# Chunks 1 to 20 of a linear attention over 12544 positions: another order of the matrix jobs within a tile

## The chip, the core and the metric

The kernel runs on one core of a Trainium2 chip. The number that counts is the device time of one execution in microseconds (us), from launch to the last store; below it is given as the median of several executions. One further execution was recorded by the hardware profiler, and everything said here about single instructions comes from that one.

The core has five engines that work side by side and wait for each other through semaphores. TensorE (PE) multiplies matrices; its weight loads are shown as PEld. VectorE (DVE), ScalarE (ACT) and GpSimd (POOL) work on elements. SyncE (SP) starts transfers from memory. Each engine carries out its own instructions in the order of its program, so an instruction that waits holds up all that stand behind it on that engine.

## The reference

Three layers on a sequence `x` of 128 rows. Nearly all the time goes into the first, a linear cross attention that reads a context of 12544 rows:

```python
k = heads(ctx @ Wk.T + bk)              # 16 heads of 32
v = heads(ctx @ Wv.T + bv)
k_prime = relu(k @ Wkf.T) * mask        # 64 features per head
kv    = sum over rows of k_prime^T v    # 64 x 32 per head
k_sum = sum over rows of k_prime
out = (q_prime @ kv) / (q_prime @ k_sum + 1e-8)
```

The other two layers, a gated recurrence and a mixture of two experts, work on 128 rows and follow behind it.

## The kernel before, in words

Every product is made from numbers split into a high and a low part, `hi` and `lo`: three matrix multiplications (`lo*hi`, `hi*lo`, `hi*hi`; the helper `three`, L773, L774, L775) add up in one place. An engine writes the high part (a copy to a shorter type, always ACT), another the low part (the difference).

The context is worked through in **chunks** of 512 rows, `c` = 0 to 24 (the last one has half a chunk), and each chunk in four **tiles** of 128 rows, `t` = 0 to 3; tile number `n` = 4c + t, 98 in all. A tile has these jobs on PE:

- **values**: 12 multiplications 512 columns wide (weights are the context, `wv` is what moves), into the bank `v_bank`. They are for the tile's own rows.
- **keys**: 12 multiplications 512 columns wide, into `k_bank`. They are one quarter `m` = t of the keys of the *next* chunk.
- four **feature jobs**, i = 0 to 3: two multiplications of 256 columns each (L855), into the two banks `f_ps[i % 2]`.
- **key_values**: 8 multiplications of 256 columns (L868), which add this tile's, or the former tile's, features times values to `kv_ps`.

The other engines' part of a tile, by names and lines of the kernel before:

- `features_share` on ACT (L546) copies half a feature bank to `fb`; `features_sum` on DVE (L1264) adds it to the other half, into `kf`, and thereby gives the bank back (`fsum_ready`). Feature job i waits until the sum of job i-2 is done, so job 2 waits for the sum of job 0 of its own tile and job 3 for that of job 1.
- `masked_features` on DVE (L1271) applies relu and mask to the 1024 features of the tile, in place in `kf`, and raises `kf_ready`. Three instructions take it from there: `add_features` on POOL (L455) adds `kf` to `ksum_acc`; `features_high` on ACT (L552) writes the high part; `features_low` on DVE (L1277) waits for that and writes the low part, which `key_values` needs.
- `values_high` on ACT (L537), `values_low` on DVE (L1255): the split of the values.
- `keys_high` on ACT (L529, two instructions), `keys_low` on DVE (L1247, two instructions): the split of the keys, which frees `k_bank`.
- `split_ctx_high` on ACT (L521) and `split_ctx_low` on POOL (L448): the split of a tile of the context two chunks ahead. POOL does, tile by tile, `split_ctx_low` and then `add_features`.

The order is written out by hand in one program per engine. A `period` is a chunk, `tile` is a tile on ACT and on DVE. Chunks 1 to 20 are a loop of two chunks per turn on PE (`Fori`); on ACT the loop ends after chunk 18 and on DVE after chunk 16, and the rest is straight code, because chunks 17 and 18 carry four small sums each on DVE (`row_sum`) and chunks 19 to 21 the splitting of weights (`qkv_high` on ACT, `qkv_low` on DVE). Inside a loop the thresholds of the waits are computed by register instructions.

Of the kernel before, what the change touches and what calls it, by code (L numbers as in the profile page):

```python
# [13 lines left out]
CHUNK = 2 * HALF  # L14
TILES = CHUNK // P
NH_CTX = S_CTX // HALF
LAST = NH_CTX // 2
# [46 lines left out]
def perceiver_kernel(nc, x_in, ctx_in, mask_in, wq_in, bq_in, wk_in, bk_in, wv_in, bv_in, bdq_in, bdk_in,  # L64
# [5 lines left out]
    with ctx:  # L70
# [438 lines left out]
        def _(act):  # L509
# [50 lines left out]
            def tile(n, t, first=False, keys=(), splits=()):  # L560

                for i in range(2):
                    features_share(n, i, first and t == 0)
                if not (first and t == 0):
# [33 lines left out]
            def period(c, s, splits=TILES, keys=CHUNK, pieces=0):  # L598
                n = TILES * c
                for t in range(TILES):  # L600
                    tile(n + t, t, keys=((c + 1, 1 - s, t, k_bank, keys),),
                         splits=((2 * c + 4 + t // 2, s, t),) if t < splits else ())
                    if pieces:
                        qkv_high(TILES * (pieces - 1) + t)

# [43 lines left out]
            period(LAST - 1, 1, splits=0, keys=HALF)  # L649
            def weight_high(g, hs=range(2)):  # L650
# [119 lines left out]
        def _(pe):  # L770
# [41 lines left out]
            def values(n, s, t, jobs):  # L812

                for job in jobs:
                    feature_job(*job)
                pe.wait_ge(v_lo_ready, n)
                for k in range(KC):
                    value_step(n, s, t, k)
# [75 lines left out]
                    if t > 0:  # L894
                        key_values(t - 1, t + 1, first=t == 1)

            def period(c, s, n_keys=CHUNK):
                n = TILES * c
                for t in range(TILES):
                    jobs = [(c, s, n + t, t, i) for i in range(JOBS)]  # L900
                    values(n + t, s, t, jobs[0:2])
                    keys(c + 1, 1 - s, t, jobs[2:4], n_keys)
                    key_values(n + t - 1, t + 1)

# [314 lines left out]
        def _(dve):  # L1219
# [73 lines left out]
            def tile(n, t, first=False, keys=()):  # L1293

                features_sum(n, t, 0, first)
                features_sum(n, t, 1, False)
                if first and t == 0:
                    queries_out()
                else:
# [46 lines left out]
            def period(c, s, keys=CHUNK, pieces=0, sums=None):  # L1346
                n = TILES * c
                for t in range(TILES):
                    if sums is not None:
                        row_sum(sums, t)  # L1350
# [3 lines left out]
                    tile(n + t, t, keys=((c + 1, 1 - s, t, k_bank, keys),))  # L1354

            def queries_out():
                for b in range(2):
# [43 lines left out]
            dve.wait_ge(mask_loaded, 16)  # L1401
            for t in range(TILES):
                tile(t, t, first=t < 2, keys=((1, 1, t, k_bank, CHUNK),))
            with dve.Fori(1, LAST - 7, 2) as c:
                period(c, 1)
                period(c + 1, 0)
            dve.wait_ge(sums_loaded, 16 * 2)
            for i in range(2):
                period(LAST - 7 + i, 1 - i, sums=i)
            period(LAST - 5, 1, pieces=1)  # L1410
            period(LAST - 4, 0, pieces=2)
            period(LAST - 3, 1, pieces=3)
            qkv_low(3 * KC - 1)
            period(LAST - 2, 0)
            period(LAST - 1, 1, keys=HALF)
# [223 lines left out]
```

## Time and profile before

| what | us |
|---|---|
| median of three executions | 860.26 (860.06 to 860.57) |
| profiled execution, its own time | 860.48 |
| its span, first to last instruction | 858.7 |
| PE busy in it | 850.4 (99%) |
| DVE, ACT, POOL busy | 679.9 (79%), 554.5 (65%), 368.9 (43%) |

The span is what the profiler shows; about 1.8 us of launch and end lie around it. "Busy" for PE counts overlapping multiplications once. A matmul's row has the time from its start to the modelled end of its result, so rows overlap; how long one holds the engine is read from the distance between two starts.

### The profile page before, as it was taken

Reading aid. Unit: us, or ns where it says so; the run is one execution under the profiler, and the core shown is the slowest. Engines: PE = TensorE matmul, PEld = TensorE weight load, DVE = VectorE, ACT = ScalarE, POOL = GpSimd, SP = SyncE. Lnnn points to the kernel's source line nnn. Section 1 sums busy time; section 2 is a strip of 40 time slices with the busy share of each in tenths; the row PEclk is TensorE's granted clock in tenths of the full one; section 3 lists DMA queues with packets and bytes.
Section 4 is the critical chain, followed back from the end, with each engine's and each line's share of the span. In section 5 each row is a group of like instructions: output and inputs, shape, how many; then the busy total and the mean of one; then the engine's idle time right before and its main releaser. Section 6 shows DMA issues by size and latency. Waiting matters only on the chain.

```text
span 858.7 us, 14381 instructions
## 1 busy us (share of the span) xinstructions
PE 850.4 (99%) x4602; PEld 729.6 (85%) x4602; DVE 679.9 (79%) x1069; ACT 554.5 (65%) x1010; POOL 368.9 (43%) x212
## 2 busy tenths in 40 slices
PE   9999999999999999999999999999999999999998
PEld 7888888888888888888888888888888889878767
DVE  5777777777777777777777777888888878879897
ACT  5666666666666666666666666666777666587563
POOL 2555454544555544454455554445445533220000
DMA  7212214010101010010101010010101000589840
GB/s 272 98 51 73 76 52 168 24 49 24 49 24 49 24 41 33 24 49 24 49 24 49 24 49 24 28 45 25 49 25 50 26 1 1 216 319 410 306 147 13
DMA packets 19529, 66.25 MB, mean 77 GB/s; under 512 B 2224, under 2 KB 2992, under 8 KB 19120
## 3 DMA queue, kind: packets, MB, share of 16 engines
q1 hardware_dynamic: 19072, 64.88, 21.3%
q10 hardware_dynamic: 432, 1.05, 0.3%
q8 instruction: 14, 0.23, 0.1%
q14 instruction: 11, 0.09, 0.0%
HBM read 65.66 MB, written 0.26 MB: 77 GB/s over the span
## 4 chain that ended last, share of the span: by engine, by line
PE 93%; issue 4%; DVE 1%; POOL 0%; DMA 0%; ACT 0%; POOLq 0%; SPq 0%; DVEq 0%; ACTq 0%
PE side_ps L773 21%; PE side_ps L774 21%; PE side_ps L775 20%; PE kv_ps L868 11%; PE side_ps L855 11%; PE kv_ps L1165 2%; PE side_ps L965 1%; PE side_ps L971 1%; PE kv_ps L1147 1%; PE side_ps L975 1%; PE side_ps L941 1%; PE side_ps L946 0%; PE side_ps L1047 0%; PE side_ps L876 0%; DVE kv_parts L1499 0%
## 5 line engine op out<-in xcount | busy, mean ns | idle before, releaser
L455 POOL TENSOR_TENSOR ksum_acc<-ksum_acc,kf 128x1024 f32<-128x1024 f32 x97 | 233.3, 2405 | 86.7 <-DVE kf L1271 86.7
L448 POOL TENSOR_TENSOR ctx_lo<-ctx_raw,ctx_hi 128x512 fp32r<-128x512 f32 x92 | 119.3, 1298 | 273.7 <-ACT ctx_hi L521 273.7
L529 ACT ACTIVATE keys<-side_ps,bias_cols 64x512 fp32r<-64x512 f32 (+1 forms) x196 | 132.3, 675 | 149.0 <-PE side_ps L775 146.5
L1247 DVE SCALAR_TENSOR_TENSOR keys<-side_ps,bias_cols,keys 64x512 fp32r<-64x512 f32 (+1 forms) x196 | 144.9, 739 | 83.9 <-ACT keys L529 80.6
L1264 DVE TENSOR_TENSOR kf<-side_ps,fb 128x256 f32<-128x256 f32 x392 | 148.6, 420 | 16.6 <-ACT fb L546 5.3
L773 PE MATMUL side_ps<-ctx_hi,wk_lo 128*128 128x512 f32 (+1 forms) x400 | 154.2, 385 | 0.0
L773 PE MATMUL side_ps<-wv_hi,ctx_lo 128*128 128x512 f32 x392 | 153.9, 393 | 0.0
L774 PE MATMUL side_ps<-wv_lo,ctx_hi 128*128 128x512 f32 x392 | 153.8, 392 | 0.0
L774 PE MATMUL side_ps<-ctx_lo,wk_hi 128*128 128x512 f32 (+1 forms) x400 | 153.6, 384 | 0.0
L775 PE MATMUL side_ps<-wv_hi,ctx_hi 128*128 128x512 f32 x392 | 152.6, 389 | 0.0
L775 PE MATMUL side_ps<-ctx_hi,wk_hi 128*128 128x512 f32 (+1 forms) x400 | 152.4, 381 | 0.0
L546 ACT ACTIVATE fb<-side_ps 128x256 f32<-128x256 f32 x392 | 129.0, 382 | 8.5 <-PE side_ps L855 6.2
L1277 DVE TENSOR_TENSOR kf<-kf 128x1024 fp32r<-128x1024 f32 x96 | 118.3, 1232 | 12.3 <-ACT kf L552 12.3
L855 PE MATMUL side_ps<-bd,keys 128*128 128x256 f32 x784 | 126.6, 283 | 0.9 <-DVE kf L1264 0.9
L855 PEld LDWEIGHTS side_ps<-bd,keys 128*128 128x128 f32 x784 | 114.8, 190 | 9.4 <-DVE kf L1264 1.3
L537 ACT ACTIVATE v<-side_ps 128x512 fp32r<-128x512 f32 x98 | 58.7, 599 | 92.4 <-PE side_ps L775 92.4
L868 PEld LDWEIGHTS kv_ps<-kf,v 128*128 128x128 f32 x784 | 106.5, 190 | 7.6 <-issue 0.5
L868 PE MATMUL kv_ps<-kf,v 128*128 128x256 f32 x784 | 109.9, 283 | 0.3 <-DVE kf L1277 0.3
L552 ACT ACTIVATE kf<-kf 128x1024 fp32r<-128x1024 f32 x96 | 102.0, 1063 | 2.0
L1255 DVE TENSOR_TENSOR v<-side_ps,v 128x512 fp32r<-128x512 f32 x98 | 67.7, 691 | 30.0 <-ACT v L537 30.0
L775 PEld LDWEIGHTS side_ps<-ctx_hi,wk_hi 128*128 128x128 f32 x400 | 75.4, 188 | 15.1
L775 PEld LDWEIGHTS side_ps<-wv_hi,ctx_hi 128*128 128x128 f32 x392 | 73.6, 188 | 16.1
(205 smaller groups left out, 954.1 us busy)
## 6 DMA issues: line engine op xcount, KB each, us to landing
ctx_raw<-in_ctx SPq DMA_DIRECT2D x46, 512.0 KB, 3.3
early<-in_stream SPq DMA_DIRECT2D x15, 1024.0 KB, 8.4
raw<-in_stream SPq DMA_DIRECT2D x12, 1024.0 KB, 9.1
early<-in_stream SPq DMA_DIRECT2D x8, 512.0 KB, 4.3
early<-in_ctx SPq DMA_DIRECT2D x2, 512.0 KB, 6.1
early<-in_wv SPq DMA_DIRECT2D x1, 1024.0 KB, 8.0
early<-in_wq SPq DMA_DIRECT2D x1, 1024.0 KB, 9.4
early<-in_wo SPq DMA_DIRECT2D x1, 1024.0 KB, 7.0
```

Source lines behind the costliest of these rows:

```text
L448: pool.tensor_tensor(ctx_lo[:, s, :, cols], raw[:, :, t % 2 * P:(t % 2 + 1) * P], ctx_hi[:, s, :, cols].bitcast(f32), ALU.subtract).then_i ...
L455: pool.tensor_tensor(ksum_acc[:, :].rearrange("p (j f) -> p j f", f=P), ksum_acc[:, :].rearrange("p (j f) -> p j f", f=P), kf[:, t % 2, :, ...
L529: act.activation(keys_2[rows, s, 2 * m + h, 0:n], src[rows, 0:n], ACT.Identity, bias=bias_cols[rows, KC + m:KC + m + 1]).then_inc(k_hi_rea ...
L546: act.activation(fb[:, i % 2, :, :], f_ps[i % 2][:, :].rearrange("p (j x f) -> p j x f", j=2, x=2) [:, :, 1, :], ACT.Copy).then_inc(fb_rea ...
L773: pe.matmul(out_ps, st_lo, mv_hi, start=start, stop=False, **kw)
L774: pe.matmul(out_ps, st_hi, mv_lo, start=False, stop=False, **kw)
L775: return pe.matmul(out_ps, st_hi, mv_hi, start=False, stop=stop, **kw)
L855: last = pe.matmul(f_ps[i % 2][:, (j % 2) * 2 * P:(j % 2 + 1) * 2 * P], keys_2[:, s, j, t * P:(t + 1) * P], bd[:, :, :].rearrange("p x f - ...
L868: return pe.matmul(kv_ps[:, j, :, :].rearrange("p x f -> p (x f)"), v_2[:, t % 2, j, :, :].rearrange("p x e -> p (x e)"), kf_2[:, t % 2, j ...
L1247: dve.scalar_tensor_tensor(out=keys_2[other, s, 2 * m + h, 0:n], in0=src[rows, 0:n], scalar=bias_cols[rows, KC + m:KC + m + 1], in1=keys_2 ...
L1264: dve.tensor_tensor(kf[:, t % 2, 2 * i:2 * i + 2, :], f_ps[i % 2][:, :].rearrange("p (j x f) -> p j x f", j=2, x=2)[:, :, 0, :], fb[:, i % ...
L1277: dve.tensor_tensor(kf_2[:, t % 2, :, 1, :], kf[:, t % 2, :, :], kf_2[:, t % 2, :, 0, :].bitcast(f32), ALU.subtract)\
```

## The change

Only the order of work in chunks 1 to 20 (tiles 4 to 83) changes. No instruction of a tile is added or taken away.

On PE a tile was: feature jobs 0 and 1, values of this tile, the first three of the twelve multiplications of keys, feature jobs 2 and 3, the other nine, key_values of the tile in front. It becomes: feature jobs 0 and 1, key_values of the tile in front, feature jobs 2 and 3, keys, values of the *next* tile. So one values job is moved ahead of the loop, and chunk 21, which has the old order, leaves out its first one.

On ACT and DVE the split of a tile's features (`features_high`, `features_low`) moves from the middle of the following tile into the tile itself: on ACT behind the split of the context, ahead of keys_high; on DVE right behind `masked_features`, ahead of `keys_low`. POOL's and SP's programs stay as they are.

```diff
@@ ScalarE @@
+            def tile_burst(n, t, keys, splits=(), piece=None):
+                features_share(n, 0, False)
+                features_share(n, 1, False)
+                values_high(n, t, False)
+                features_share(n, 2, False)
+                features_share(n, 3, False)
+                for x in splits:
+                    split_ctx_high(*x)
+                if piece is not None:
+                    qkv_high(piece)
+                features_high(n, t)
+                keys_high(*keys)
...
+            features_high(TILES - 1, TILES - 1)
             with act.Fori(1, LAST - 5, 2) as c:
-                period(c, 1)
-                period(c + 1, 0)
+                period_burst(c, 1)
+                period_burst(c + 1, 0)
...
-            period(LAST - 5, 1, pieces=1)
-            period(LAST - 4, 0, pieces=2)
-            period(LAST - 3, 1, pieces=3)
+            period_burst(LAST - 5, 1, pieces=1)
+            period_burst(LAST - 4, 0, pieces=2)
+            period(LAST - 3, 1, pieces=3, behind_burst=True)
@@ TensorE @@
+            def period_burst(c, s):
+                n = TILES * c
+                for t in range(TILES):
+                    for i in (0, 1):
+                        feature_job(c, s, n + t, t, i)
+                    key_values(n + t - 1, t + 1)
+                    for i in (2, 3):
+                        feature_job(c, s, n + t, t, i)
+                    keys(c + 1, 1 - s, t, ())
+                    if t < TILES - 1:
+                        values(n + t + 1, s, t + 1, ())
+                    else:
+                        values(n + t + 1, 1 - s, 0, ())
...
             period_0()
+            values(TILES, 1, 0, ())
             with pe.Fori(1, LAST - 3, 2) as c:
-                period(c, 1)
-                period(c + 1, 0)
-            period(LAST - 3, 1)
+                period_burst(c, 1)
+                period_burst(c + 1, 0)
+            period(LAST - 3, 1, behind_burst=True)
@@ VectorE @@
+            def tile_burst(n, t, keys, between=None):
+                features_sum(n, t, 0, False)
+                features_sum(n, t, 1, False)
+                values_low(n, t)
+                features_sum(n, t, 2, False)
+                features_sum(n, t, 3, False)
+                masked_features(n, t)
+                if between is not None:
+                    between()
+                features_low(n, t)
+                keys_low(*keys)
```

`between` is the `row_sum` of chunks 17 and 18 or the `qkv_low` of chunks 19 and 20, which stood ahead of the tile.

The order of instructions shows it at two places. First PE, inside the loop of chunks 1 to 20 of the kernel before, from the end of one tile into the next; `kf_2,v_2` is key_values, `bd,keys_2` a feature job, `wv` values, `wk` keys:

```order
L868 MATMUL kv_ps<-kf_2,v_2 128x256 [waits kf_lo_ready,v_lo_ready]
L868 MATMUL kv_ps<-kf_2,v_2 128x256 x7
L853 ISA
L855 MATMUL side_ps<-bd,keys_2 128x256 [waits fsum_ready]
L855 MATMUL side_ps<-bd,keys_2 128x256
L855 MATMUL side_ps<-bd,keys_2 128x256 [waits fsum_ready]
L855 MATMUL side_ps<-bd,keys_2 128x256
L773 MATMUL side_ps<-wv_hi,ctx_lo 128x512 [waits v_lo_ready]
```

The same place in the changed kernel, from feature job 0 (its second multiplication is the first row here) to the first of the keys:

```order
L877 MATMUL side_ps<-bd,keys_2 128x256
L877 MATMUL side_ps<-bd,keys_2 128x256 [waits fsum_ready]
L877 MATMUL side_ps<-bd,keys_2 128x256
L890 MATMUL kv_ps<-kf_2,v_2 128x256 [waits kf_lo_ready,v_lo_ready]
L890 MATMUL kv_ps<-kf_2,v_2 128x256 x7
L875 REGISTER_ALU
L877 MATMUL side_ps<-bd,keys_2 128x256 [waits fsum_ready]
L877 MATMUL side_ps<-bd,keys_2 128x256
L875 REGISTER_ALU
L877 MATMUL side_ps<-bd,keys_2 128x256 [waits fsum_ready]
L877 MATMUL side_ps<-bd,keys_2 128x256
L814 ISA [waits ctx_lo_ready]
```

Between feature jobs 0, 1 and feature jobs 2, 3 there now lie the eight multiplications of key_values alone, where there were values and three multiplications of keys; all sixteen multiplications of 256 columns stand in one row.

Second DVE, inside its loop of the kernel before, from the low part of the former tile's features (L1277) to the low part of the keys (L1247); L1271 is `masked_features`:

```order
L1277 TENSOR_TENSOR kf_2<-kf,kf_2 128x8x128 [waits kf_hi_ready]
L1254 REGISTER_ALU
L1255 TENSOR_TENSOR v_2<-side_ps,v_2 128x8x64 [waits v_hi_ready]
L1263 REGISTER_ALU
L1264 TENSOR_TENSOR kf<-side_ps,fb 128x256 [waits fb_ready]
L1263 REGISTER_ALU
L1264 TENSOR_TENSOR kf<-side_ps,fb 128x256 [waits fb_ready]
L1271 REGISTER_ALU [waits fsum_ready]
L1271 TENSOR_SCALAR kf<-kf,mask 128x1024
L1245 ISA
L1247 SCALAR_TENSOR_TENSOR keys_2<-side_ps,bias_cols,keys_2 64x512 [waits k_hi_ready]
```

The same stretch of the changed kernel, from `values_low` (L1297) on; L1306 is `features_sum`, L1313 `masked_features`, L1319 `features_low`, L1289 `keys_low`:

```order
L1297 TENSOR_TENSOR v_2<-side_ps,v_2 128x8x64 [waits v_hi_ready]
L1305 REGISTER_ALU
L1306 TENSOR_TENSOR kf<-side_ps,fb 128x256 [waits fb_ready]
L1305 REGISTER_ALU
L1306 TENSOR_TENSOR kf<-side_ps,fb 128x256 [waits fb_ready]
L1313 REGISTER_ALU [waits fsum_ready]
L1313 TENSOR_SCALAR kf<-kf,mask 128x1024
L1319 TENSOR_TENSOR kf_2<-kf,kf_2 128x8x128 [waits kf_hi_ready]
L1287 ISA
L1289 SCALAR_TENSOR_TENSOR keys_2<-side_ps,bias_cols,keys_2 64x512 [waits k_hi_ready]
```

The low part of the features now stands directly behind the mask of its own tile, and the low part of the keys stands behind it.

## Rows read from the trace of the kernel before

**Rows 1.** The page, busy time of each engine, its share, instructions

```profile
PE 850.4 (99%) x4602; PEld 729.6 (85%) x4602; DVE 679.9 (79%) x1069; ACT 554.5 (65%) x1010; POOL 368.9 (43%) x212
```

**Rows 2.** Timeline of PE, one tile: start, us, what, how many merged

```profile
302.92 0.64 PE L855 MATMUL side_ps<-bd,keys 128*128 128x256 f32 x4
303.39 0.40 PE L773 MATMUL side_ps<-ctx_hi,wk_lo 128*128 128x512 f32 x1
...
305.46 1.11 PE L868 MATMUL kv_ps<-kf,v 128*128 128x256 f32 x8
306.41 0.64 PE L855 MATMUL side_ps<-bd,keys 128*128 128x256 f32 x4
306.89 0.40 PE L773 MATMUL side_ps<-wv_hi,ctx_lo 128*128 128x512 f32 x1
...
309.64 0.39 PE L773 MATMUL side_ps<-ctx_hi,wk_lo 128*128 128x512 f32 x1
...
310.32 0.28 PE L855 MATMUL side_ps<-bd,keys 128*128 128x256 f32 x1
```

**Rows 3.** Timeline of DVE, the same stretch

```profile
306.38 1.53 DVE L1247 SCALAR_TENSOR_TENSOR keys<-side_ps,bias_cols,keys 64x512 fp32r<-64x512 f32 x2 [0.88 <-ACT keys L529]
...
308.86 1.23 DVE L1277 TENSOR_TENSOR kf<-kf 128x1024 fp32r<-128x1024 f32 x1 [0.16 <-ACT kf L552]
...
311.26 0.76 DVE L1264 TENSOR_TENSOR kf<-side_ps,fb 128x256 f32<-128x256 f32 x2
312.15 0.75 DVE L1271 TENSOR_SCALAR kf<-kf,mask 128x1024 f32<-128x1024 f32 x1
```

**Rows 4.** Timeline of ACT, the same stretch

```profile
307.76 1.06 ACT L552 ACTIVATE kf<-kf 128x1024 fp32r<-128x1024 f32 x1
...
310.33 0.62 ACT L521 ACTIVATE ctx_hi<-ctx_raw 128x512 fp32r<-128x512 f32 x1
310.86 0.65 ACT L546 ACTIVATE fb<-side_ps 128x256 f32<-128x256 f32 x2
```

**Rows 5.** Timeline of POOL, the same stretch

```profile
311.04 1.29 POOL L448 TENSOR_TENSOR ctx_lo<-ctx_raw,ctx_hi 128x512 fp32r<-128x512 f32 x1 [3.05 <-ACT ctx_hi L521]
312.98 2.41 POOL L455 TENSOR_TENSOR ksum_acc<-ksum_acc,kf 128x1024 f32<-128x1024 f32 x1 [0.65 <-DVE kf L1271]
```

**Rows 6.** Timeline of chunk 0, a feature job and an idle ACT behind it

```profile
27.09 0.48 PE L855 MATMUL side_ps<-bd,keys 128*128 128x256 f32 x2
...
27.61 0.38 ACT L546 ACTIVATE fb<-side_ps 128x256 f32<-128x256 f32 x1 [2.26 <-PE side_ps L855]
```

**Rows 7.** Timeline of chunk 0, where feature jobs of tile 1 waited for sums

```profile
31.55 0.64 ACT L546 ACTIVATE fb<-side_ps 128x256 f32<-128x256 f32 x2
...
31.95 0.76 DVE L1264 TENSOR_TENSOR kf<-side_ps,fb 128x256 f32<-128x256 f32 x2 [1.70 <-ACT fb L546]
...
32.42 0.63 PEld L855 LDWEIGHTS side_ps<-bd,keys 128*128 128x128 f32 x4 [1.35 <-DVE kf L1264]
...
32.74 0.81 DVE L1271 TENSOR_SCALAR kf<-kf,mask 128x1024 f32<-128x1024 f32 x1
...
33.10 0.39 PE L773 MATMUL side_ps<-wv_hi,ctx_lo 128*128 128x512 f32 x1
```

**Rows 8.** Timelines of DVE and POOL, features_low beside add_features, chunk 23

```profile
714.34 1.45 DVE L1277 TENSOR_TENSOR kf<-kf 128x1024 fp32r<-128x1024 f32 x1 [0.30 <-ACT kf L552]
...
712.29 2.41 POOL L455 TENSOR_TENSOR ksum_acc<-ksum_acc,kf 128x1024 f32<-128x1024 f32 x1 [4.89 <-DVE kf L1271]
```

**Rows 9.** Timelines of DVE and POOL, the mask beside the split, chunk 19

```profile
600.65 0.82 DVE L1271 TENSOR_SCALAR kf<-kf,mask 128x1024 f32<-128x1024 f32 x1
...
599.63 1.30 POOL L448 TENSOR_TENSOR ctx_lo<-ctx_raw,ctx_hi 128x512 fp32r<-128x512 f32 x1 [3.06 <-ACT ctx_hi L521]
```

**Rows 10.** Timelines of DVE and POOL, the two halves of the split of `wv`

```profile
18.38 1.23 DVE L1391 TENSOR_TENSOR wv_lo<-early,wv_hi 128x1024 fp32r<-128x1024 f32 x1 [0.31 <-ACT wv_hi L630]
...
18.43 3.40 POOL L470 TENSOR_TENSOR wv_lo<-early,wv_hi 128x1024 fp32r<-128x1024 f32 x1 [6.13 <-ACT wv_hi L630]
```

More of the change, by code:

```diff
@@ L558, in features_high_half, with tile @@
                 act.activation(kf_2[:, t, js, 0, :], kf[:, t, js, :], ACT.Copy).then_inc(kf_hi_ready, 1)
-            def tile(n, t, first=False, keys=(), splits=()):
+            def tile_burst(n, t, keys, splits=(), piece=None):
[10 more added lines that the diff above has]
+                keys_high(*keys)
+            def tile(n, t, first=False, keys=(), splits=(), former=True):
                 for i in range(2):
                     features_share(n, i, first and t == 0)
-                if not (first and t == 0):
+                if former and not (first and t == 0):
                     features_high(n - 1, t - 1)
@@ L601, in period @@
                     tile(n + t, t, keys=((c + 1, 1 - s, t, k_bank, keys),),
-                         splits=((2 * c + 4 + t // 2, s, t),) if t < splits else ())
+                         splits=((2 * c + 4 + t // 2, s, t),) if t < splits else (),
+                         former=t > 0 or not behind_burst)
                     if pieces:
@@ L895, in period_0, with period @@
                         key_values(t - 1, t + 1, first=t == 1)
-            def period(c, s, n_keys=CHUNK):
+            def period_burst(c, s):
+                n = TILES * c
+                for t in range(TILES):
+                    for i in (0, 1):
[8 more added lines that the diff above has]
+                        values(n + t + 1, 1 - s, 0, ())
+            def period(c, s, n_keys=CHUNK, behind_burst=False):
                 n = TILES * c
@@ L900, in period @@
                     jobs = [(c, s, n + t, t, i) for i in range(JOBS)]
-                    values(n + t, s, t, jobs[0:2])
+                    if t == 0 and behind_burst:
+                        for job in jobs[0:2]:
+                            feature_job(*job)
+                    else:
+                        values(n + t, s, t, jobs[0:2])
                     keys(c + 1, 1 - s, t, jobs[2:4], n_keys)
@@ L1291, in masked_features_last, with tile @@
                    .then_inc(kf_ready, 1)
-            def tile(n, t, first=False, keys=()):
+            def tile_burst(n, t, keys, between=None):
[9 more added lines that the diff above has]
+                keys_low(*keys)
+            def tile(n, t, first=False, keys=(), former=True):
                 features_sum(n, t, 0, first)
@@ L1298, in tile @@
                     queries_out()
-                else:
+                elif former:
                     features_low(n - 1, t - 1)
@@ L1344, in row_sum, with period_burst, period @@
                    .then_inc(row_sums_ready, 1)
-            def period(c, s, keys=CHUNK, pieces=0, sums=None):
+            def period_burst(c, s, pieces=0, sums=None):
                 n = TILES * c
                 for t in range(TILES):
+                    i = TILES * (pieces - 1) + t
+                    between = None
                     if sums is not None:
-                        row_sum(sums, t)
+                        between = lambda t=t: row_sum(sums, t)
+                    elif pieces and i:
+                        between = lambda i=i: qkv_low(i - 1)
+                    tile_burst(n + t, t, (c + 1, 1 - s, t, k_bank, CHUNK), between)
+            def period(c, s, keys=CHUNK, pieces=0, behind_burst=False):
+                n = TILES * c
+                for t in range(TILES):
                     i = TILES * (pieces - 1) + t
@@ L1353, in period @@
                         qkv_low(i - 1)
-                    tile(n + t, t, keys=((c + 1, 1 - s, t, k_bank, keys),))
+                    tile(n + t, t, keys=((c + 1, 1 - s, t, k_bank, keys),), former=t > 0 or not behind_burst)
             def queries_out():
@@ L1403, in _ @@
                 tile(t, t, first=t < 2, keys=((1, 1, t, k_bank, CHUNK),))
+            features_low(TILES - 1, TILES - 1)
             with dve.Fori(1, LAST - 7, 2) as c:
-                period(c, 1)
-                period(c + 1, 0)
+                period_burst(c, 1)
+                period_burst(c + 1, 0)
             dve.wait_ge(sums_loaded, 16 * 2)
             for i in range(2):
[L1409 to L1412, printed above, removed]
+                period_burst(LAST - 7 + i, 1 - i, sums=i)
+            period_burst(LAST - 5, 1, pieces=1)
+            period_burst(LAST - 4, 0, pieces=2)
+            period(LAST - 3, 1, pieces=3, behind_burst=True)
             qkv_low(3 * KC - 1)
```

5 lines of the change are left out of this document (4 added, 1 removed).

## The prediction

> **What bounds the kernel now.** I read the page's busy times first: PE is busy for 99% of the span, the others for 43% to 79% [rows 1]. A gain must therefore come out of PE's own stream, and a loss can come from any engine that makes PE wait. So I read the timeline of one tile, PE first and then DVE, ACT and POOL. On PE look at the distances between starts: the tile goes from 302.92 to 310.32, 7.40 us, without a gap [rows 2]. Values take 2.75 us (306.89 to 309.64), the first three keys 0.68 (to 310.32), which is 0.227 for one wide multiplication. Feature jobs 2 and 3 take 0.47 (302.92 to 303.39), the other nine keys 2.07, key_values 0.95, feature jobs 0 and 1 0.48. On the other engines look at who is where when: POOL's add_features begins right behind the mask (312.90 to 312.98), and DVE's features_low of a tile begins only 3.4 us behind the end of that tile's mask (at 308.86; the mask one period ahead of the one shown ended at 312.90 - 7.40 = 305.50), when the add of 2.41 us is over [rows 3, 5]. The mask in its turn begins when POOL's split has less than 0.2 us left (312.15 against 311.04 + 1.29 = 312.33).
>
> **PE's own stream.** At 0.227 each, twelve wide multiplications would take 2.72 us and nine 2.04, yet they take 2.75 and 2.07 [rows 2]: behind narrow ones the wide ones lose 0.03 us. The first narrow ones win about 0.01 back (0.47 against 0.48 for four). A switch from wide to narrow and back thus costs about 0.02 us. There were two in a tile and there is one now: 0.02 less, 7.38 instead of 7.40. Over 80 tiles that is 1.6 us. This is all that PE itself can give.
>
> **A short wait.** A feature job waits for the sum that frees its bank. Feature jobs 2 and 3 need the sums of jobs 0 and 1, and only key_values (0.95) lies between them now. Count from the start of job 0. Its second multiplication starts at 0.11 and lasts 0.28, and ACT begins 0.04 after such an end (27.57 to 27.61 [rows 6]): 0.43, or up to 0.50 with a register instruction that stands ahead of it. The copy takes 0.38, DVE follows 0.03 later (31.55 + 0.38 to 31.95, rounded), and a pair of sums takes 0.76 [rows 7]: done at 1.60 to 1.67. In chunk 0 the wide multiplication behind such a pair of feature jobs started 0.39 after the pair of sums ended (32.71 to 33.10 [rows 7]). That makes the keys start at 1.99 to 2.06. Unhindered they would start at 0.47 + 0.95 + 0.48 = 1.90. So if nothing else waited, a tile would take 7.38 + 0.09 to 0.16, up to 7.54.
>
> **The long wait.** features_low is moved in beside add_features. Three places show what DVE and POOL do to each other.
> - features_low takes 1.23 alone [rows 3]. At 714.34 it took 1.45, while POOL's add ran from 712.29 to 714.70: it ended 1.09 after the add [rows 8]. With 0.36 of overlap it lost 0.22; had both gone on at half speed it would have lost 0.18. It looks held from an early point until POOL was done.
> - The mask takes 0.75 alone. At 600.65 it took 0.82 and ended 0.54 after POOL's split (600.93) [rows 3, 9].
> - The other way round: DVE began a subtraction at 18.38 and POOL one of the same size at 18.43. DVE took its usual 1.23; POOL ended 2.22 after it, at 3.40 in place of about 2.41 [rows 5, 10].
>
> So whoever begins first keeps the other out, to about 0.2 us. The Trainium skill has this as a rule, in "SBUF — State Buffer", section "Who interferes with whom": a DVE instruction with two SBUF inputs, or in a two-port mode, and a GpSimd instruction that reads SBUF take a lock for the whole instruction, and the later one is fully blocked. By that rule features_low waits out the whole add; the trace agrees, as far as 0.4 us of overlap can show. The sum below comes out as the rule has it; an even sharing would give some 930 us.
>
> Now the new tile, counted from DVE's first sum. The pair of sums ends at 0.76, the keys start at 1.15 (+0.39), the last feature multiplication starts 0.12 ahead of them and ends at 1.31, ACT's fourth copy runs from 1.35 to 1.73. DVE's last sum ends near 2.20, and the mask begins 0.13 after a sum in the loop (312.02 to 312.15 [rows 3]): at 2.32. ACT's split of the context starts about 0.27 behind the start of that copy (a pair takes 0.65, one 0.38), runs 1.63 to 2.25, and POOL's half begins 0.08 later (310.95 to 311.04 [rows 4, 5]): at 2.33. Mask and split come within 0.01 of each other. Both orders end alike:
> - *Mask first.* It ends at M = 3.08. The split is held and ends at M + 1.30 - 0.19 = 4.19; the add stands ready behind it and runs 4.15 to 6.56. ACT's features_high, 1.06 [rows 4], lets features_low ask at M + 0.03 + 1.06 + 0.03 = 4.20 (0.03 for each hand-over, as from ACT to DVE in [rows 7]), 0.05 too late. It ends at 6.56 + 1.09 = 7.65, keys_low (0.03 + 1.53 [rows 3]) at 9.21, and the next first sum starts at 9.24.
> - *Split first.* It ends at 3.63, the mask at 4.17, the add runs 4.25 to 6.66, features_low ends at 7.75, the next first sum starts at 9.34.
>
> PE would be ready earlier (keys and values from 1.15 end at 1.15 + 5.47 = 6.62), so DVE sets the period: 9.24 or 9.34 for 7.40. Behind the blocked features_low stand keys_low and the sums; PE waits for them, first at key_values and then at feature jobs 2 and 3. ACT, 65% busy now [rows 1], has room.
>
> **The sum.** 80 tiles x 1.84 = 147 us with the mask first, 155 with the split first. In chunks 17 to 20 DVE's code is straight; the mask then follows a sum at 0.04 in place of 0.13 (32.71 to 32.74 [rows 7]), 16 x -0.09 = -1.4. In seven tiles of chunks 19 and 20 qkv_low, of half features_low's size, comes in between; I estimate 0.4 each, 3 us. row_sum lies in time that DVE waits anyway. The old span and rim, 860.5 by the profiled run (0.2 over the median), give 860.5 + 147 + 3 - 1 = 1009, or 1017. I take the first, since the mask was ahead by a hair: **1009 us**; the likeliest case's own range is 1000 to 1022.
>
> **The rivals.**
> - *The split isn't held by the mask.* Only the mask was seen waiting, never POOL for a mask. Then the split ends at 3.63 though the mask ended at 3.08, the add runs 3.60 to 6.01, features_low ends at 7.10, the period is 8.69: 80 x 1.29 = 103, 963 us. Speaks for it: no row shows the reverse. Against: the wv rows show POOL held by another DVE instruction.
> - *features_low gets in ahead of the add.* It was 0.05 late with the mask first, less than what I can place. Then it ends at 5.43, the add at 7.65 and keys_low at 6.99, ahead of the next sums: only the short wait is left. 80 x 0.14 = 11, **871 us**.
> - *No wait at all, the other side.* The sums of jobs 0 and 1 come in time behind key_values, and features_low too. It holds if that pair of sums ends by 1.90 - 0.39 = 1.51 after job 0's start; my count is 1.60 at least. The price is -1.6 us: 858.9, which is a gain of 0.19%, not to be told from none.
>
> **How the numbers follow.** The long wait with either order 0.74; split not held 0.09; features_low first 0.12; no wait 0.03; the rest 0.02, a mixture or sharing at half speed (7.65 becomes 6.7, the period 8.3, some 930). The range takes in the first two, 0.83: 958 to 1022. A measurement of this kernel tells about 0.2% from no change: faster 0.02 (no wait, and a little more than counted), same 0.03, slower 0.95.
>
> **What the changed profile would show.** Right: features_low at a mean near 3.5 us instead of 1.23, ending about 1.09 after each add; PE busy near 7.4 of each 9.2 us, its idle time put down to DVE's sums and kf; the period steady. The share of masks near 1.85 us against 0.75 tells how often the split was first. Wrong: features_low near 1.23 with add_features at 3.5 (the second rival); features_low near 2.5 and its end not tied to the add (sharing); wide multiplications that lose more or less than 0.03 behind the sixteen narrow ones. What would upset it most is a shift of 0.1 us between mask, split and add, since order alone decides there.

## The result, and the profile after

The changed kernel takes **1015.83 us** (median of five runs, 1014.61 to 1017.81) against 860.26 (860.06 to 860.57): a ratio of 1.1812, with a 95% interval of 1.1799 to 1.1824. The profiled execution took 1016.83 us, its span is 1015.0.

The page of the changed kernel, first its busy times, then the chain that ended last by engine, then the costliest group (how often | busy us, mean ns | idle before and what ended it):

```profile
PE 900.8 (89%) x4602; PEld 748.4 (74%) x4602; DVE 859.4 (85%) x1069; ACT 563.6 (56%) x1010; POOL 399.9 (39%) x212
...
DVE 52%; PE 27%; ACT 11%; issue 8%; DVEq 0%; POOL 0%; DMA 0%; POOLq 0%; SPq 0%; ACTq 0%
...
L1319 DVE TENSOR_TENSOR kf<-kf 128x1024 fp32r<-128x1024 f32 x96 | 288.0, 3000 | 79.7 <-ACT kf L552 79.7
```

The timeline of DVE, one tile, and the mask and features_low of the next:

```profile
402.13 0.76 DVE L1306 TENSOR_TENSOR kf<-side_ps,fb 128x256 f32<-128x256 f32 x2
...
404.46 0.75 DVE L1313 TENSOR_SCALAR kf<-kf,mask 128x1024 f32<-128x1024 f32 x1
406.34 3.46 DVE L1319 TENSOR_TENSOR kf<-kf 128x1024 fp32r<-128x1024 f32 x1 [1.13 <-ACT kf L552]
409.83 1.53 DVE L1289 SCALAR_TENSOR_TENSOR keys<-side_ps,bias_cols,keys 64x512 fp32r<-64x512 f32 x2
411.39 0.76 DVE L1306 TENSOR_TENSOR kf<-side_ps,fb 128x256 f32<-128x256 f32 x2
...
413.83 1.88 DVE L1313 TENSOR_SCALAR kf<-kf,mask 128x1024 f32<-128x1024 f32 x1 [0.24 <-DVE kf L1306]
416.83 2.43 DVE L1319 TENSOR_TENSOR kf<-kf 128x1024 fp32r<-128x1024 f32 x1 [1.13 <-ACT kf L552]
```

The timeline of POOL over the same two tiles:

```profile
404.61 1.76 POOL L448 TENSOR_TENSOR ctx_lo<-ctx_raw,ctx_hi 128x512 fp32r<-128x512 f32 x1 [5.14 <-ACT ctx_hi L521]
406.33 2.38 POOL L455 TENSOR_TENSOR ksum_acc<-ksum_acc,kf 128x1024 f32<-128x1024 f32 x1
413.86 1.30 POOL L448 TENSOR_TENSOR ctx_lo<-ctx_raw,ctx_hi 128x512 fp32r<-128x512 f32 x1 [5.15 <-ACT ctx_hi L521]
415.79 2.39 POOL L455 TENSOR_TENSOR ksum_acc<-ksum_acc,kf 128x1024 f32<-128x1024 f32 x1 [0.63 <-DVE kf L1313]
```

Read the two together. In the first tile the mask is short (0.75) and the split long (1.76 for the 1.29 of [rows 5]): the mask was first. The add begins at 406.33, features_low at 406.34, and features_low ends at 409.80, which is 1.09 after the add. In the second tile the split is short (1.30) and the mask long (1.88): the split was the one that went ahead, and features_low ends 1.08 after the add again. From first sum to first sum the tile takes 9.26 us (402.13 to 411.39).

The timeline of PE, the same tile, and of ACT its split of the context:

```profile
402.61 0.83 PE L877 MATMUL side_ps<-bd,keys 128*128 128x256 f32 x4 [0.74 <-DVE kf L1306]
403.29 0.40 PE L795 MATMUL side_ps<-ctx_hi,wk_lo 128*128 128x512 f32 x1
...
408.75 0.63 PE L877 MATMUL side_ps<-bd,keys 128*128 128x256 f32 x4
409.95 1.18 PE L890 MATMUL kv_ps<-kf,v 128*128 128x256 f32 x8 [0.56 <-DVE kf L1319]
```

```profile
403.90 0.63 ACT L521 ACTIVATE ctx_hi<-ctx_raw 128x512 fp32r<-128x512 f32 x1
```

Where [rows 2] had no gap, PE now waits twice in a tile: for features_low ahead of key_values, and for the sums of feature jobs 0 and 1 (which stand behind keys_low) ahead of feature jobs 2 and 3. Keys and values, 403.29 to 408.75, take 5.46 us in a row.

**The balance.** The time of tile n is counted from mask n-1 to mask n. The tiles of the changed chunks read: 9.25 to 9.28 where the mask was first; once in eight tiles, where the split was first, a pair of about 9.38 and 9.36 (9.62 and 9.12 the first time, and twice 9.64 as the second); 9.16 to 9.18 in tiles 68 to 77; 9.62 (once 9.92) in tiles 78 to 83. The split was first in nine of the 80 tiles: tile 4, and then 10, 18 and so on to 66. From mask 3 to mask 86 it is 770.97 us, before 614.20 (83 x 7.40): 156.8 more, which is the whole difference of the two profiled executions (1016.83 - 860.48 = 156.35, with 0.4 given back elsewhere).

### The profile page after: what moved, and what is told of

It is laid out like the page before. It is cut to its first block, busy times and chain, and to the rows that moved or that the text cites. A ratio compares the mean times of both kernels' runs of the same rounds, so it can differ in the third digit from the quotient of the medians.

```text
span 1015.0 us, 14362 instructions
## 1 busy us (share of the span) xinstructions
PE 900.8 (89%) x4602; PEld 748.4 (74%) x4602; DVE 859.4 (85%) x1069; ACT 563.6 (56%) x1010; POOL 399.9 (39%) x212
## 4 chain that ended last, share of the span: by engine, by line
DVE 52%; PE 27%; ACT 11%; issue 8%; DVEq 0%; POOL 0%; DMA 0%; POOLq 0%; SPq 0%; ACTq 0%
DVE kf L1319 26%; DVE keys L1289 10%; PE side_ps L877 8%; ACT kf L552 8%; DVE kf L1306 7%; DVE kf L1313 7%; PE side_ps L795 3%; PE side_ps L796 3%; ACT fb L546 3%; PE side_ps L797 3%; PE kv_ps L890 2%; PE kv_ps L1207 2%; DVE w_lo L1394 1%; PE side_ps L1006 1%; PE side_ps L1012 1%
## 5 line engine op out<-in xcount | busy, mean ns | idle before, releaser
L1319 DVE TENSOR_TENSOR kf<-kf 128x1024 fp32r<-128x1024 f32 x96 | 288.0, 3000 | 79.7 <-ACT kf L552 79.7
L448 POOL TENSOR_TENSOR ctx_lo<-ctx_raw,ctx_hi 128x512 fp32r<-128x512 f32 x92 | 150.7, 1638 | 442.9 <-ACT ctx_hi L521 442.9
L546 ACT ACTIVATE fb<-side_ps 128x256 f32<-128x256 f32 x392 | 134.5, 383 | 289.0 <-PE side_ps L877 288.4
L877 PE MATMUL side_ps<-bd,keys 128*128 128x256 f32 x784 | 142.7, 303 | 58.3 <-DVE kf L1306 58.3
L877 PEld LDWEIGHTS side_ps<-bd,keys 128*128 128x128 f32 x784 | 118.9, 190 | 85.9 <-DVE kf L1306 74.0
L1306 DVE TENSOR_TENSOR kf<-side_ps,fb 128x256 f32<-128x256 f32 x392 | 149.1, 420 | 16.9 <-ACT fb L546 6.5
L1289 DVE SCALAR_TENSOR_TENSOR keys<-side_ps,bias_cols,keys 64x512 fp32r<-64x512 f32 (+1 forms) x196 | 144.8, 739 | 20.2 <-ACT keys L529 14.3
L890 PE MATMUL kv_ps<-kf,v 128*128 128x256 f32 x784 | 115.1, 289 | 46.3 <-DVE kf L1319 46.3
L890 PEld LDWEIGHTS kv_ps<-kf,v 128*128 128x128 f32 x784 | 100.2, 189 | 60.4 <-issue 59.5
L1313 DVE TENSOR_SCALAR kf<-kf,mask 128x1024 f32<-128x1024 f32 x97 | 83.5, 861 | 10.5 <-DVE kf L1306 2.2
L795 PEld LDWEIGHTS side_ps<-ctx_hi,wk_lo 128*128 128x128 f32 x400 | 77.5, 194 | 15.4 <-issue 3.2
L796 PEld LDWEIGHTS side_ps<-ctx_lo,wk_hi 128*128 128x128 f32 x400 | 77.3, 193 | 12.1 <-issue 0.5
```

Of the source, the lines that this page charges most:

```text
L546: act.activation(fb[:, i % 2, :, :], f_ps[i % 2][:, :].rearrange("p (j x f) -> p j x f", j=2, x=2) [:, :, 1, :], ACT.Copy).then_inc(fb_rea ...
L795: pe.matmul(out_ps, st_lo, mv_hi, start=start, stop=False, **kw)
L796: pe.matmul(out_ps, st_hi, mv_lo, start=False, stop=False, **kw)
L877: last = pe.matmul(f_ps[i % 2][:, (j % 2) * 2 * P:(j % 2 + 1) * 2 * P], keys_2[:, s, j, t * P:(t + 1) * P], bd[:, :, :].rearrange("p x f - ...
L890: return pe.matmul(kv_ps[:, j, :, :].rearrange("p x f -> p (x f)"), v_2[:, t % 2, j, :, :].rearrange("p x e -> p (x e)"), kf_2[:, t % 2, j ...
L1289: dve.scalar_tensor_tensor(out=keys_2[other, s, 2 * m + h, 0:n], in0=src[rows, 0:n], scalar=bias_cols[rows, KC + m:KC + m + 1], in1=keys_2 ...
```

## The experiments

All of them change the changed kernel; "tile" is the time from mask to mask. Each ratio is against the kernel before, executed beside that experiment (860.37 for experiments 1 to 4, 860.20 for 5 to 8).

**1. The keys' low part ahead of features_low.** If POOL's add keeps features_low out, then DVE can do something useful meanwhile, and the tile shrinks though the same instructions run.

```diff
                 if between is not None:
                     between()
-                features_low(n, t)
                 keys_low(*keys)
+                features_low(n, t)
```

> Edit: on VectorE, in the tiles of chunks 1 to 20, keys_low stands ahead of features_low. Theory 1 (features_low is held until GpSimd's add is over, and that hold is what VectorE's period is made of): keys_low (1.56 us) now runs inside the add's time, features_low asks late and still ends 1.09 after the add, so key_values waits for it; with keys start K after a tile's first feature job, the mask ends at K + 1.95, the add at K + 5.42, features_low at K + 6.51, and a tile takes 8.1 us: about 917 us in all, 912 to 926. Theory 2 (the close order on TensorE, feature jobs 2 and 3 right behind key_values, makes the loss): no change against the changed kernel, 1010 to 1020. Theory 3 (VectorE's idle 1.13 us between mask and features_low, waiting for ScalarE, is the loss and the add doesn't matter): that idle time is filled, features_low takes 1.23, and the time falls to the short wait alone, 866 to 875.

Measured: 941.21 us, ratio 1.0940 (1.0918 to 1.0961). The tile is 8.26. The timelines of DVE, POOL and PE:

```profile
408.29 1.53 DVE L1289 SCALAR_TENSOR_TENSOR keys<-side_ps,bias_cols,keys 64x512 fp32r<-64x512 f32 x2 [1.70 <-ACT keys L529]
409.85 1.34 DVE L1319 TENSOR_TENSOR kf<-kf 128x1024 fp32r<-128x1024 f32 x1
411.22 0.76 DVE L1306 TENSOR_TENSOR kf<-side_ps,fb 128x256 f32<-128x256 f32 x2
...
413.22 0.76 DVE L1306 TENSOR_TENSOR kf<-side_ps,fb 128x256 f32<-128x256 f32 x2 [0.65 <-ACT fb L546]
```

```profile
407.70 2.41 POOL L455 TENSOR_TENSOR ksum_acc<-ksum_acc,kf 128x1024 f32<-128x1024 f32 x1
```

```profile
411.34 1.19 PE L890 MATMUL kv_ps<-kf,v 128*128 128x256 f32 x8 [0.66 <-DVE kf L1319]
```

features_low comes at 409.85, when the add (to 410.11) has 0.26 left, and takes 1.34: it ends 1.08 after the add, as always. So the long record belongs to the meeting with the add, not to the new place as such. keys_low, which reads one operand from a matrix bank (`side_ps`), lies wholly beside the add and takes its usual 1.53: the add doesn't hold every instruction of DVE. The direction was right, the size was not: I had 8.1 for the tile and 912 to 926 us in all. features_low now ends 0.03 before the sums begin, so key_values starts late, feature jobs 2 and 3 behind it too, and the second pair of sums waits 0.65. That gives 8.26, and once in eight tiles, where the split was first, 8.37 and then 9.23.

**2. No add beside it.** POOL adds 2 of the 1024 columns; the rest of that running sum is left out.

```diff
+            def add_one(n, t):
...
+                pool.tensor_tensor(ksum_acc[:, 0:2], ksum_acc[:, 0:2], kf[:, t % 2, 0, 0:2], ALU.add)\
+                    .then_inc(ksum_added, 1)
...
-                    add_features(n + t, t)
+                    add(n + t, t)
```

> Edit: in chunks 1 to 20 GpSimd's add_features adds 2 of the 1024 columns, with the same waits and signals; the rest of that sum is left out. Theory 1: features_low takes 1.23 again, only the short wait of feature jobs 2 and 3 is left (0.07 to 0.14 us a tile against before), and in one tile of eight, where the split is first, a further 0.6 us: 866 to 877 us, most likely 871. Theory 2 and theory 3: GpSimd's add has nothing to do with it, 1010 to 1020.

Measured: 879.61 us, ratio 1.0224 (1.0203 to 1.0244). The group of features_low, over all 96:

```profile
L1325 DVE TENSOR_TENSOR kf<-kf 128x1024 fp32r<-128x1024 f32 x96 | 120.5, 1255 | 79.7 <-ACT kf L558 79.7
```

features_low takes 1.26, the tile 7.53. Of the 156 us, 136 are gone with one instruction per tile on an engine that the chain gives 0%. The time lies above the range that I had given (866 to 877); experiment 3, which does too, shows why.

**3. The add behind features_low.** The same, but with the whole computation: POOL's add waits for features_low.

```diff
                     if t < splits:
                         split_ctx_low(2 * c + 4 + t // 2, s, t)
+                    if behind_low:
+                        pool.wait_ge(kf_lo_ready, n + t + 1)
                     add_features(n + t, t)
```

> Edit: in chunks 1 to 20 GpSimd's add_features waits for kf_lo_ready of its own tile as well, so that it starts behind features_low. Nothing is left out. Theory 1: as without the add, 866 to 877 us, most likely 871; features_low at 1.23, add_features at 2.40, TensorE's tile at 7.47 to 7.54. Theories 2 and 3: 1010 to 1020.

Measured: 880.77 us, ratio 1.0235 (1.0218 to 1.0252). The timelines of DVE, POOL and PE:

```profile
406.32 1.23 DVE L1321 TENSOR_TENSOR kf<-kf 128x1024 fp32r<-128x1024 f32 x1 [1.13 <-ACT kf L554]
```

```profile
407.63 2.40 POOL L455 TENSOR_TENSOR ksum_acc<-ksum_acc,kf 128x1024 f32<-128x1024 f32 x1 [1.28 <-DVE kf L1321]
```

```profile
401.19 0.64 PE L879 MATMUL side_ps<-bd,keys 128*128 128x256 f32 x4
...
402.62 0.81 PE L879 MATMUL side_ps<-bd,keys 128*128 128x256 f32 x4
403.27 0.40 PE L797 MATMUL side_ps<-ctx_hi,wk_lo 128*128 128x512 f32 x1
```

The add does all its work and features_low has its 1.23 again. So it isn't the work on POOL, it is where it lies. What is left is the short wait: feature jobs 2 and 3 take 0.65 from start to the keys' start in place of 0.47, the keys start 2.08 behind job 0, the tile is 7.55. The mask still meets the split: once in eight tiles the split wins, the mask takes 1.87, and the pair takes 7.66 and 8.14. This is 10 us worse than the likeliest value that I had expected, and above the range. Against the kernel before, 80 tiles at about 0.15 make 12 us, the nine tiles where the split wins about 6, and tiles 84 and 85, at the border to the unchanged chunk 21, 1.7 (8.92 and 7.58 for twice 7.40).

**4. PE in its old order, ACT and DVE in the new one.** It undoes the PE half of the change.

```diff
-            values(TILES, 1, 0, ())
             with pe.Fori(1, LAST - 3, 2) as c:
-                period_burst(c, 1)
-                period_burst(c + 1, 0)
-            period(LAST - 3, 1, behind_burst=True)
+                period(c, 1)
+                period(c + 1, 0)
+            period(LAST - 3, 1)
```

> Edit: TensorE has the order of the kernel before in all chunks; ScalarE and VectorE have the changed order. Theory 1: VectorE's round (two sums, values_low, two sums, mask, the hold, features_low, keys_low) has the same parts, since the second pair of sums again follows the first by way of TensorE: 9.24 to 9.34 us a tile, 1009 to 1018 us. Theory 2: the burst is gone and the time is near that of before, 858 to 872. Theory 3: about as theory 1.

Measured: 1043.59 us, ratio 1.2129 (1.2105 to 1.2154). The timelines of DVE and PE, the waits, and a window (PE, PEld, DVE, ACT, POOL busy, then PEclk):

```profile
408.23 3.48 DVE L1318 TENSOR_TENSOR kf<-kf 128x1024 fp32r<-128x1024 f32 x1 [1.13 <-ACT kf L552]
```

```profile
413.33 0.69 PE L795 MATMUL side_ps<-ctx_hi,wk_lo 128*128 128x512 f32 x1 [1.85 <-DVE keys L1288]
413.82 0.63 PE L796 MATMUL side_ps<-ctx_lo,wk_hi 128*128 128x512 f32 x1
414.25 0.63 PE L797 MATMUL side_ps<-ctx_hi,wk_hi 128*128 128x512 f32 x1
```

```profile
PE side_ps L795 <- DVE keys L1288: 123.8, 79, 2.2
```

```profile
413.30:417.00 3.70, 3.67 (x11) 3.09 (x12) 2.47 (x6) 1.40 (x3) 0.12 (x1) 0.54 0.00 0
```

The long wait (3.48) is there without PE's new order, so the loss comes from the move on DVE and ACT. But it is worse than both of my figures. The old order asks for the keys' bank sooner, while keys_low stands behind the blocked features_low (1.85 us here, 123.8 in 79 times), and feature jobs 2 and 3 come only behind the first three keys: 9.51 per tile. After some of these idle stretches PE is granted half its clock: the window above has 0.54, and wide multiplications start 0.43 apart instead of 0.23. Many of these tiles take 9.8 to 10.4 (with a qkv_low up to 10.8), some lose nothing. The mean granted clock of 0.962 over 1042 us makes some 79 us at the 1.2 GHz level.

**5. The split behind the mask as well.** Experiment 3, and POOL's split waits for the mask.

```diff
+                    if behind_low:
+                        pool.wait_ge(kf_ready, n + t + 1)
                     if t < splits:
                         split_ctx_low(2 * c + 4 + t // 2, s, t)
+                    if behind_low:
+                        pool.wait_ge(kf_lo_ready, n + t + 1)
```

> Edit on top of e3: GpSimd's split_ctx_low of a tile waits for kf_ready of that tile too, so the mask is always first. Nothing is left out. Theory (the order of mask and split costs 0.8 us in the one tile of eight where the split came first in e3, and nothing else is left but the short wait of feature jobs 2 and 3, 7.55 us a tile): ten tiles save 0.8 each, 880.8 - 8 = 873, 871 to 875. Rival (those tiles are slow because of the loop's end, not because of the order): 880 to 882.

Measured: 874.01 us, ratio 1.0160 (1.0144 to 1.0175). POOL and DVE:

```profile
408.35 1.29 POOL L448 TENSOR_TENSOR ctx_lo<-ctx_raw,ctx_hi 128x512 fp32r<-128x512 f32 x1 [2.77 <-DVE kf L1317]
```

```profile
409.32 1.40 DVE L1323 TENSOR_TENSOR kf<-kf 128x1024 fp32r<-128x1024 f32 x1 [1.13 <-ACT kf L556]
```

The split now begins 0.16 behind the end of the mask and still runs when features_low asks, which costs that one 0.17 (1.40 for 1.23) and nobody else. The pair of 7.66 and 8.14 has become 7.65 and 7.42, twice the normal tile of 7.53. Of the 6.8 us between experiments 3 and 5, those pairs make 5.8 (8 times 0.73), and tile 5, behind the first tile where the split had won, 0.6 (7.53 for 8.12). This is the best version that computes everything, and it still loses 13.8 us to the kernel before: some 10 by the short wait (0.13 a tile), 1.7 at tiles 84 and 85 (8.95 and 7.57), and nearly 1 in eight tiles with a row_sum (7.62 to 7.69).

**6. Sums at half size.** Experiment 5, and the copies and sums of feature jobs 0 and 1 handle half their columns; the other half is left out. This takes the short wait away and shows what PE's order is worth.

```diff
-                features_share(n, 0, False)
-                features_share(n, 1, False)
+                features_share_half(n, 0)
+                features_share_half(n, 1)
...
-                features_sum(n, t, 0, False)
-                features_sum(n, t, 1, False)
+                features_sum_half(n, t, 0)
+                features_sum_half(n, t, 1)
```

> Edit on top of e5: the copies and sums of feature jobs 0 and 1 in chunks 1 to 20 take one of their two blocks, 128 columns of 256; the other half of those sums is left out. Theory (the short wait is the time from feature job 0 to the end of the second sum, less key_values): the pair of sums ends about 0.2 to 0.3 us earlier, nothing waits any more and a tile takes 24 wide and 16 narrow multiplications with one switch, 7.38: 860.3 - 1.6 = 858.7, up to 861 if a few hundredths of the wait are left. Rival (TensorE pays for sixteen narrow multiplications in a row, or the switch isn't what the 0.03 us are): 862 or more, with no wait in the trace.

Measured: 860.71 us (11 runs) against 860.20, ratio 1.0004 (0.9995 to 1.0013). The timeline of PE, one tile, and a wait in chunk 21:

```profile
404.55 0.64 PE L888 MATMUL side_ps<-bd,keys 128*128 128x256 f32 x4
...
406.46 0.40 PE L806 MATMUL side_ps<-ctx_hi,wk_lo 128*128 128x512 f32 x1
...
411.93 0.64 PE L888 MATMUL side_ps<-bd,keys 128*128 128x256 f32 x4
...
650.99 0.80 PE L888 MATMUL side_ps<-bd,keys 128*128 128x256 f32 x4 [0.97 <-DVE kf L1317]
```

404.55 to 411.93 is 7.38, without a gap: the 0.02 for a switch is there. 80 of them are 1.6 us, yet the time is not shorter. It is given back where chunk 21 takes up the old order: tile 84 takes 8.93, with PE waits of 0.37 ahead of keys and 0.97 ahead of a feature job, and tile 85 7.57, together 1.7 more than before. The rival value of 862 and up is not met, nor is a gain. The time lies in the range that I had given (up to 861), but I had meant the upper end for leftovers of the wait, not for this border: that is luck.

**7. Something that only writes.** Experiment 2, and POOL fills the other 1022 columns with zeros beside features_low.

```diff
-                    .then_inc(ksum_added, 1)
+                pool.memset(ksum_acc[:, 2:NF], 0.0).then_inc(ksum_added, 1)
```

> Edit on top of e2: behind the addition of 2 columns GpSimd fills the other 1022 columns with zeros (0.95 us, it writes and reads nothing); the sum is left out. It begins within 0.1 us of features_low. Theory (what excludes the other engine is reading the on-chip memory, not being busy): features_low stays at 1.23 to 1.26 and the time at that of e2, 879 to 881. Rival (any GpSimd instruction holds VectorE): features_low at about 2.1, up to 70 us more, some 930 to 950.

Measured: 879.45 us (one run), against 879.61 in experiment 2. DVE and POOL:

```profile
405.47 1.25 DVE L1325 TENSOR_TENSOR kf<-kf 128x1024 fp32r<-128x1024 f32 x1 [1.13 <-ACT kf L558]
```

```profile
405.58 0.95 POOL L463 MEMSET ksum_acc<- 128x1022 f32 x1
```

The fill lies beside features_low over its whole 0.95, and neither costs the other anything. But here features_low was first, so this says only that it doesn't keep the fill out. For the other order the changed kernel itself has one place, in chunk 23, where POOL fills another tile:

```profile
889.59 1.22 DVE L1319 TENSOR_TENSOR kf<-kf 128x1024 fp32r<-128x1024 f32 x1
...
889.38 0.95 POOL L486 MEMSET read_k<- 128x1024 f32 x1
```

The fill has 0.74 left when features_low begins, and that one takes 1.22. So an instruction of POOL that only writes doesn't shut DVE out; the add and the split, which read, do. SBUF is the on-chip memory in which `kf`, `kf_2`, `ksum_acc` and the context tiles lie; the matrix banks (`side_ps`, `kv_ps`) are not part of it. The Trainium skill, "SBUF — State Buffer", section "Who interferes with whom", says the same: a DVE instruction with two SBUF inputs contends with a GpSimd instruction that reads SBUF, not with one that only writes it. The traces agree for features_low: 1.25 and 1.22 beside a fill, 3.46 beside the add.

**8. Job 0's sum by DVE alone.** Experiment 5, and DVE sums feature job 0 in one reduction that reads both halves out of the bank, without ACT's copy ahead. It was to shorten the short wait with the whole computation in place.

```diff
-                features_share(n, 0, False)
-                features_share(n, 1, False)
+                features_share_behind(n, 1)
...
-                features_sum(n, t, 0, False)
+                features_sum_alone(n, t, 0)
```

> Edit on top of e5: the sum of feature job 0 in chunks 1 to 20 is made by VectorE alone, as a reduction over the two halves that reads 512 numbers (about 0.69 us) in place of ScalarE's copy and a sum; job 1 is then the first copy of ScalarE. Nothing is left out. Theory: the reduction runs 0.44 to 1.13 after the tile's first feature job, the copy of job 1 is ready at 1.10, its sum ends at 1.50, just under the 1.51 at which feature job 3 would wait: 7.38 to 7.42 us a tile, 859 to 862 us, a tie with the kernel before. Rival (VectorE, now with 0.27 us more a tile, becomes the bound, or the pair ends as late as in e5): 866 to 880.

Measured: 879.82 us, ratio 1.0231 (1.0217 to 1.0245). PE and DVE:

```profile
399.69 0.64 PE L887 MATMUL side_ps<-bd,keys 128*128 128x256 f32 x4
```

```profile
399.49 0.75 DVE L1299 SCALAR_TENSOR_TENSOR keys<-side_ps,bias_cols,keys 64x512 fp32r<-64x512 f32 x1
400.28 0.69 DVE L1326 TENSOR_REDUCE kf<-side_ps 128x256 f32<-128x512 f32 x1
401.00 0.42 DVE L1316 TENSOR_TENSOR kf<-side_ps,fb 128x256 f32<-128x256 f32 x1
```

The reduction starts 0.59 behind job 0, not 0.44 as I had counted, and takes 0.69: the pair of sums ends 1.73 behind job 0, no sooner than with the copy (1.69 in experiment 5). The reduction isn't late by a hand-over: DVE is at keys_low until 400.24 and goes on to it within 0.04. With the longer sum DVE has no slack left ahead of its sums and sets the tile, 7.60. The rival was right.

## Why the prediction was right

The forecast was 1009 us with 958 to 1022 around it; 1015.8 was measured, by the mechanism named. Where the sum is 8 us short is told below, and one of its choices, the order of mask and split, was right by luck.

**PE's own stream: right.** 7.38 per tile was forecast, and 7.38 stands in experiment 6.

**The short wait: right, slightly short.** The keys start 2.08 behind job 0 (forecast 1.99 to 2.06), the tile is 7.55 in experiment 3 and 7.53 in experiment 5 (7.47 to 7.54).

**The long wait: right.** features_low was to end 1.09 after the add: 1.08 in every tile that was read, whether the two met for 2.4 us or for 0.26. [rows 8] had shown only 0.36 of overlap; the rule holds over the whole add. Experiments 2 and 3 take the meeting away in two ways, and 136 and 135 us go with it. "Split not held" fell with the 1.76 of the splits, "features_low ahead of the add" with the start of features_low, 0.01 behind the add's. The forecast had 0.05 there: the split that the mask holds ends 1.16 after the mask (406.37 against 405.21), not 1.11, and the add behind it starts that much later. Whether the order hung on that 0.01 is not shown; the mask was held even where its record began 0.03 first. "No wait" would have needed what experiment 6 forced.

**The mask and the split: right in result, wrong in one step.** The mask starts 2.33 behind the first sum (forecast 2.32). POOL's split starts at 2.48, not 2.33. I had let ACT's split of the context begin inside the last copy (1.63); it began at 1.77 (402.13 to 403.90). So "within 0.01 of each other" was really 0.15, and the mask is first nearly always. Of the two totals, 1009 was rightly taken, but on the strength of a gap of 0.01 that wasn't the real one: that choice was luck. The exception is one tile in eight, at the same place of each turn of the loops: there the mask starts 0.24 behind the sums instead of 0.13 and the split gets in. What delays DVE by 0.11 there the trace does not say; it stays open. But the change didn't bring it: the kernel before has the same 0.24 once in eight tiles, where I had read only the 0.13 of [rows 3]. Its timeline of DVE, such a tile:

```profile
401.06 0.75 DVE L1271 TENSOR_SCALAR kf<-kf,mask 128x1024 f32<-128x1024 f32 x1 [0.24 <-DVE kf L1264]
```

**The sum: 149 forecast, 156.8 measured.** By stretches, against 7.40 a tile:
- Tiles 5 to 67: +119.8; 63 x 1.84 is 115.9. The other 3.9 us: a tile of 9.265 and not 9.24 (1.6), eight pairs that take 18.73 and not 18.53 (1.6), and two tiles of 9.64 where the granted clock fell (0.6).
- Tiles 68 to 76: +16.0; forecast 9 x (1.84 - 0.09) = 15.8.
- Tiles 77 to 83: +15.4; 12.3 for the seven, 2.7 for six with a qkv_low (0.45 each, estimated 0.4), 0.3 for one with the lower clock.
- Tile 4: +0.4 where I had 1.84.
- Tiles 84 and 85: +5.2, **of which the sum has only the 0.4 of the seventh qkv_low**. I looked at the inside of the changed chunks and left out the seam. In chunk 21 PE is back in the old order and needs the keys' bank at once, while DVE's keys_low stands behind the last blocked features_low.

The lower clock stands nowhere in the forecast; within the tiles it cost the 0.9 named above.

The timeline of PE of the changed kernel at that seam:

```profile
803.74 0.47 PE L795 MATMUL side_ps<-ctx_hi,wk_lo 128*128 128x512 f32 x1 [2.50 <-DVE keys L1289]
...
805.33 0.91 PE L877 MATMUL side_ps<-bd,keys 128*128 128x256 f32 x4 [0.66 <-DVE kf L1306]
```

And DVE and POOL in a tile with qkv_low (L1394) just before:

```profile
796.90 1.79 DVE L1394 TENSOR_TENSOR w_lo<-early,w_lo 128x512 fp32r<-128x512 f32 x1
798.61 3.42 DVE L1319 TENSOR_TENSOR kf<-kf 128x1024 fp32r<-128x1024 f32 x1
```

```profile
796.47 1.67 POOL L448 TENSOR_TENSOR ctx_lo<-ctx_raw,ctx_hi 128x512 fp32r<-128x512 f32 x1 [5.14 <-ACT ctx_hi L521]
798.10 2.84 POOL L455 TENSOR_TENSOR ksum_acc<-ksum_acc,kf 128x1024 f32<-128x1024 f32 x1
```

Here the two engines lock each other out in turn: the mask holds the split, the split holds qkv_low (1.79), qkv_low holds the add (2.84 for 2.41), and the add holds features_low.

**What the change could give at most** is 1.6 us, and not even that shows while chunk 21 keeps the old order. With the long wait gone, the reordering still loses, mostly by the short wait (874.0, experiment 5): no placing of POOL's work tried here rescues it.

## What to carry to other kernels

Before an instruction that reads two operands from SBUF, or one like the mask that works in place there, moves on DVE, look at what POOL reads at the new place: the later of the two waits for the whole of the earlier, and no semaphore, wait or chain shows it, only a record longer than its mean elsewhere. Where two such instructions start within some 0.1 us of each other, cost both orders, and make the order certain by a wait if one of them is dear: it was worth 6.8 us between experiments 3 and 5. A delay of 0.1 us that comes once in eight tiles is enough to turn the order, so read such starts over a whole turn of a loop and not in one tile. And put the seams to the neighbouring, unchanged stages into the sum: they cost 5.2 us here, and all of the gain in experiment 6.

## What the runs showed of the hardware

- **The record that starts first doesn't always win.** In the tile at 413.83 the mask's record starts 0.03 before the split's, and yet the mask is the held one (1.88, the split 1.30). With 0.09 between them (experiment 1, mask 405.84, split 405.93) the mask won. The two share no tile, so this isn't about two engines at the same data.
- **The held one ends a fixed time after the holder:** features_low 1.08 of its 1.23, the mask 0.55 of its 0.75 (413.86 + 1.30 to 413.83 + 1.88), however long it was held.
- **PE's granted clock fell at waits under 1 us.** In the changed kernel, whose PE is busy for 89% of the span, it fell five times: at the seam, behind waits of 2.50 and 0.66, and four times in its tiles, where PE waits 0.79 to 0.95 for features_low and 0.74 for the sums, with 1.19 us of key_values between them. Three of these tiles lost about 0.3 us, one nothing. Other tiles with waits as long kept the full clock (at 419.41, 0.79 and 0.74), so the waits alone don't tell where it falls. In experiment 4, whose waits for the keys' bank are mostly 1.8 to 2.2, it fell 23 times. In the kernel before and in the experiments other than 4 the mean reads 1.00.

A window of the changed kernel behind such a pair of waits (columns as in experiment 4):

```profile
198.00:201.50 3.50, 3.45 (x10) 2.88 (x11) 2.53 (x5) 1.92 (x4) 1.17 (x1) 0.54 0.00 0
```

It lies at the lower level, 1.2 GHz, for nearly its whole length.
